# Decoder middle by token half, later helical end and second experts' opening in another order: one core of Trainium2

## The reference, cut to what matters

```python
x = x + cross_attention(layernorm(x), ctx)               # 257 keys per sequence, gelu instead of softmax
x = x + rwkv(layernorm(x))
x = x + experts0(layernorm(x))                           # 1 shared and 7 routed, two chosen
x = x + decoder(layernorm(x), ctx)                       # below
x = x + helical_attention(layernorm(x))                  # 16 heads
x = x + experts1(layernorm(x))                           # 16 experts, three chosen

def decoder(y, Z):
    y = layernorm(y + attention(y, y, y, causal=True), g1, beta1)
    y = layernorm(y + attention(y, Z, Z), g2, beta2)
    return layernorm(y + relu(y @ w1 + b1) @ w2 + b2, g3, beta3)
```

## Time and profile before

| what | us |
|---|---|
| median of three runs | 596.7 |
| the profiled execution, its own time | 599.34 |
| its span | 597.5 |
| first experts end, decoder begins | 243 |
| helical units begin | 330 |
| second norm half of the second experts turned | 468.6 |
| first `down` of the second experts | 496.7 |
| the steps' last product, then the end | 591.8, 597.5 |
| PE / DVE / ACT / POOL busy | 458 / 424 / 299 / 103 |

### The profile page before, as it was taken

The page is one execution under the profiler, slowest core; times in us unless marked ns, Lnnn a source line. Parts: engine busy times, 40 slices in busy tenths (PEclk is TensorE's granted clock), DMA queues, the critical chain, the costliest instruction groups (busy, mean ns, idle before and its releaser), DMA issues.

```text
span 597.5 us, 8935 instructions
## 1 busy us (share of the span) xinstructions
PE 458.3 (77%) x2922; PEld 346.8 (58%) x2939; DVE 423.7 (71%) x1013; ACT 299.4 (50%) x555; POOL 103.4 (17%) x104
## 2 busy tenths in 40 slices
PE   5754233999999999454667789999864349999996
PEld 2331232777787777342434678888763327777774
DVE  3369856777777776546879797878765457888885
ACT  4135031777666665232222566765632107777774
POOL 1000012222111220000044211222100320332220
PEclk9867555999999999755877989999985559999999
DMA  8930001110111100000000000000001000111101
GB/s 318 420 148 0 0 1 53 54 43 11 53 53 53 53 15 2 0 0 1 2 0 2 2 1 2 2 2 1 2 1 35 21 20 31 37 39 66 35 0 36
DMA packets 7422, 24.08 MB, mean 40 GB/s; under 512 B 774, under 2 KB 2998, under 8 KB 7260
## 3 DMA queue, kind: packets, MB, share of 16 engines
q1 hardware_dynamic: 7388, 23.63, 10.8%
HBM read 23.11 MB, written 0.52 MB: 40 GB/s over the span
## 4 chain that ended last, share of the span: by engine, by line
PE 58%; DVE 19%; issue 8%; ACT 7%; DMA 3%; SPq 2%; POOL 1%; DVEq 0%; POOLq 0%; ACTq 0%
PE pair L321 13%; PE pair L323 13%; PE pair L322 13%; DMA mb<-in_mb 3%; PE turn L315 2%; PE pair L640 2%; PE turn L321 1%; DVE st L1129 1%; PE pair L372 1%; DVE work L1313 1%; PE turn L322 1%; DVE arena L1480 1%; PE turn L323 1%; SPq L280 1%; ACT YT L762 1%
## 5 line engine op out<-in xcount | busy, mean ns | idle before, releaser
L994 ACT ACTIVATE work<-pair,vec 128x512 f32<-128x512 f32 x64 | 44.0, 688 | 39.1 <-PE pair L323 33.2
L321 PE MATMUL pair<-yTh,wh 128*128 128x512 f32 x128 | 61.4, 480 | 0.0
L1581 DVE TENSOR_TENSOR pair<-work,turn 128x512 f32<-128x512 f32 x64 | 44.5, 696 | 20.2 <-ACT work L994 18.9
L322 PE MATMUL pair<-yTl,wh 128*128 128x512 f32 x128 | 51.4, 401 | 0.0
L323 PE MATMUL pair<-yTh,wl 128*128 128x512 f32 x128 | 51.3, 401 | 0.0
L1351 DVE TENSOR_TENSOR pair<-work,pair 128x512 f32<-128x512 f32 x48 | 33.4, 696 | 24.1 <-PE pair L323 23.4
L1042 POOL TENSOR_TENSOR wl<-wraw,wh 128x512 fp32r<-128x512 f32 x24 | 30.9, 1291 | 99.3 <-ACT wh L831 99.3
L852 ACT ACTIVATE ph<-pair 128x512 fp32r<-128x512 f32 x48 | 28.7, 599 | 27.4 <-DVE pair L1351 27.4
L839 ACT ACTIVATE work<-pair 128x512 f32<-128x512 f32 x64 | 38.2, 598 | 4.8 <-PE pair L323 3.6
L321 PE MATMUL pair<-ph,wh 128*128 128x512 f32 x96 | 38.2, 398 | 1.1 <-DVE pl L1369 0.8
L640 PE MATMUL pair<-arena 64*128 64x128 f32 x512 | 34.8, 289 | 4.7 <-ACT work L918 4.5
(11 more groups left out here) (276 smaller groups left out, 1239.2 us busy)
## 6 DMA issues: line engine op xcount, KB each, us to landing
wraw<-in_w SPq DMA_DIRECT2D x8, 768.0 KB, 4.2
arena<-in_zT SPq DMA_DIRECT2D x8, 514.0 KB, 10.3
arena<-in_z SPq DMA_DIRECT2D x8, 512.0 KB, 11.1
wraw<-in_w SPq DMA_DIRECT2D x8, 512.0 KB, 3.2
mat<-in_mat SPq DMA_DIRECT2D x1, 2571.5 KB, 18.8
row<-in_row SPq DMA_DIRECT2D x1, 576.0 KB, 18.6
X<-in_x SPq DMA_DIRECT2D x1, 512.0 KB, 4.1
out_x<-X SPq DMA_DIRECT2D x2, 256.0 KB, 2.5
```

The costliest lines, as they stand in the source:

```text
L321: pe.matmul(out, ah, bh, start=start, stop=False)
L322: pe.matmul(out, ah, bl, start=False, stop=False)
L994: act.activation(act_out[q % 2], UP1[q % 4], ACT.Relu, bias=vec[:, bass.ds(at, 1)])\
L1581: dve.tensor_tensor(UP1[q % 4], act_out[q % 2], bank[h], ALU.mult).then_inc(m["mul"], 1)
```

## The change

In the decoder, norms 1 and 2 are made for each half by itself. Half 0 starts cross-attention while half 1 is normalised between tiles 0 and 2; half 1 is turned at tile 2; half 0 is normalised and turned again behind tiles 6 and 7. POOL's helical preparation starts as soon as the decoder's opening norm is done. At the helical end unit 7's two score passes come ahead of unit 6's softmax sum and weighing, and the first half's last norm is split into statistics and a later rest. In the second experts the logits are made by half into another bank, the first three `up` come before the gates, the bias product comes behind the gates' transposes, and ACT makes the gates' float copy. `route` (L370) is cut into `logits` and `turn_gates`; `cross` calls the function it is given behind `turn_probs(t)` on PE, and between `result(t - 2)` and `top(t + 2)` on DVE. The diff, cut to its core:

```diff
@@ PE
             def moe1():
-                pe.wait_ge(m_g3, 4)
-                pe.wait_ge(y_lo, 6)
-                for h in range(2):
-                    pe.matmul(acc[h], mb2[:, :], g3f[:, h * HN:(h + 1) * HN], start=True, stop=False)
                 pe.sem_inc(m["down"], FREE1["down"])
...
+                pe.wait_ge(y_lo, 6)
                 for q in range(3):
                     up(0, q)
+                pe.wait_ge(m_shift, 2)
+                for h in range(2):
+                    pe.matmul(acc[h], zerob[:, :], g3b[:, h * HN:(h + 1) * HN], start=True, stop=False)
+                turn_gates(3 * NE1, 1)
+                for h in range(2):
+                    pe.wait_ge(m_g3, 3 + h)
+                    spread(0, 2 * h)
+                for h in range(2):
+                    pe.wait_ge(m_gf, h + 1)
+                    pe.matmul(acc[h], mb2[:, :], g3f[:, h * HN:(h + 1) * HN], start=False, stop=False)
...
-            pe.wait_ge(feat_ready, n)
-            pe.wait_ge(a_y2, 2)
-            cross(1)
+            def other_turns(t):
+                if t == 2:
+                    pe.wait_ge(feat_ready, turn_half(1))
+                if t == NT:
+                    turn_half(0)
+            pe.wait_ge(feat_ready, turn_half(0))
+            cross(1, other_turns)
...
-                if u >= 2:
+                if u >= 2 and u != 8:
                     turn_weights(u - 2)
                 if 1 <= u <= len(HEL):
                     score(u - 1, 0)
+                if u == 8:
+                    turn_weights(6)
+                    score(7, 1)
...
-                if u == 9:
-                    pe.wait_ge(h_o, 7)
-                    turn4(lambda i: Y[:, i, :])
-                    pe.wait_ge(feat_ready, 18)
                 if u >= 2:
                     weigh_values(u - 2)
-                if 1 <= u <= len(HEL):
+                if 1 <= u < len(HEL):
                     score(u - 1, 1)
...
-            pe.wait_ge(h_x, 2)
-            n = turn4(lambda i: Y[:, HT + i, :])
-            pe.wait_ge(feat_ready, n)
-            route("gate", NE1, 3 * NE1, 1)
+            for h in range(2):
+                if h == 1:
+                    pe.wait_ge(h_x, 2)
+                n = turn4(lambda i: Y[:, h * HT + i, :])
+                pe.wait_ge(feat_ready, n)
+                logits("gate", NE1, 1, range(h * HT, (h + 1) * HT))
             moe1()
@@ ACT
                                accum_out=ssum[:, t:t + 1]).then_inc(c_probs, 1)
-            inverse_std(0, 1)
+                if t == 2:
+                    copy_turned(yt(1))
+            inverse_std(0)
...
-                    if h == 1 and f == 0:
-                        inverse_std(0)
+                    if f == 0:
+                        inverse_std(1 - h)
...
+                if u == 8:
+                    extract(7, 0)
...
+            for h in range(2):
+                act.wait_ge(m_g3, 3 + h)
+                c = slice(h * HN, (h + 1) * HN)
+                act.activation(g3f[:, c], g3b[0:3 * NE1, c], ACT.Copy).then_inc(m_gf, 1)
@@ POOL
-            pool.wait_ge(f_h, 1)
+            pool.wait_ge(tok_ready, 8)
@@ DVE
-                    if call == 1:
-                        dve.tensor_copy(g3f[:, c], src)
...
-            layernorm((0, 1), Y2, Y2, lambda h: affine(h, Y2, "g1", "be1").then_inc(tok_ready, 1))
-            dve.wait_ge(tok_ready, 12)
-            cross(1)
-            layernorm((0, 1), Y2, Y2, lambda h: affine(h, Y2, "g2", "be2").then_inc(tok_ready, 1))
+            norm1(0, attended(0))
+            var[1] = attended(1)
+            def other_norms(t):
+                if t == 0:
+                    norm1(1, var[1])
+                if t == 6:
+                    dve.wait_ge(c_x, NT + HT)
+                    norm2(0, statistics((0,), Y2))
+            cross(1, other_norms)
+            norm2(1, statistics((1,), Y2))
...
+                if u == 8:
+                    extract(7, 0)
                 if u >= 2:
                     softmax_sum(u - 2)
+                if u == 9:
+                    var[0] = statistics((0,), X)
...
+                if u == 8:
+                    extract(7, 1)
+                    softmax_shift(7)
                 if u >= 2:
                     result(u - 2)
...
-                if u == 8:
-                    layernorm((0,), X, Y)
+            normal((0,), X, Y, var[0])
             add_out(1)
```

More of the change, by code:

```diff
@@ L323, in mm3, with cross @@
                 return pe.matmul(out, al, bh, start=False, stop=stop)
-            def cross(call):
+            def cross(call, between=None):
                 def scores(t):
@@ L364, in cross @@
                         turn_probs(t)
+                    if between is not None:
+                        between(t)
                     if t + 2 < NT:
@@ L368, in cross, with logits, turn_gates @@
                         weigh(t - 1)
-            def route(name, ne, rows, call):
-                for t in range(NT):
-                    last = pe.matmul(bank[2][:, t * NE1:t * NE1 + ne], blk(YT, t), mcol(name), start=True, stop=True)
+            def logits(name, ne, call, tiles):
+                for t in tiles:
+                    last = pe.matmul(LOGITS[call][:, t * NE1:t * NE1 + ne], blk(YT, t), mcol(name), start=True, stop=True)
                 last.then_inc(m_logits, 1)
+            def turn_gates(rows, call):
+                pe.wait_ge(m_parts, call + 1)
                 for h in range(2):
-                    pe.wait_ge(m_parts, call + 1)
                     for i in range(HT):
-                        last = pe.transpose(blk(bank[3 + h].bitcast(BF16), i)[0:rows, :],
+                        last = pe.transpose(blk(GATES_T[call][h].bitcast(BF16), i)[0:rows, :],
                                             parts_of(rows // 3)[:, h * HT + i, :], identb[:, :])
@@ L492, in body @@
                         if not last or q + 3 < len(STEPS1):
+                            if (q + 3) % NF1 == 0:
+                                spread(i, q + 3)
                             up(i, q + 3)
@@ L534, in _ @@
             pe.wait_ge(feat_ready, n)
-            route("router", NE0 - 1, 3 * NE0, 0)
+            logits("router", NE0 - 1, 0, range(NT))
+            turn_gates(3 * NE0, 0)
             moe0()
@@ L875, in _ @@
                                           scale=scale, accum_out=ssum[:, t:t + 1])
[L876 to L881, removed]
+                last.then_inc(tok_ready, 1)
+                if h == 0:
+                    copy_turned(spT(0))
+            copy_turned(spT(1))
+            inverse_std(0)
+            copy_turned(yt(0))
+            inverse_std(1)
             for t in range(NT):
@@ L1250, in routing_parts, with add_experts @@
                     dve.wait_ge(m_gT, 2 * call + h + 1)
-                    src = bank[3 + h].bitcast(BF16)[0:3 * w, 0:HN]
+                    src = GATES_T[call][h].bitcast(BF16)[0:3 * w, 0:HN]
                     c = slice(h * HN, (h + 1) * HN)
-                    if call == 1:
-                        dve.tensor_copy(g3f[:, c], src)
                     dve.tensor_copy(g3b[0:3 * w, c], src).then_inc(m_g3, 1)
-            def moe_end(m):
-                for h in range(2):
-                    dve.wait_ge(m["back"], h + 1)
-                    dve.tensor_tensor(half(X, h), bank[2 + h], half(X, h), ALU.add).then_inc(m["x"], 1)
+            def add_experts(m, h):
+                dve.wait_ge(m["back"], h + 1)
+                dve.tensor_tensor(half(X, h), bank[2 + h], half(X, h), ALU.add).then_inc(m["x"], 1)
             dve.wait_ge(x_loaded, 16)
@@ L1376, in _ @@
             bodies(dve, NE0 // 2, body0)
-            moe_end(m)
-            dve.wait_ge(m["x"], 2)
-            layernorm((0, 1), X, Y)
+            var = [0, 0]
+            for h in range(2):
+                add_experts(m, h)
+                dve.wait_ge(m["x"], h + 1)
+                var[h] = statistics((h,), X)
+            for h in range(2):
+                normal((h,), X, Y, var[h])
             for h in range(2):
@@ L1390, in _, with attended @@
                 hs = slice(h * HT, (h + 1) * HT)
-                dve.wait_ge(a_prob, h + 1)
-                dve.sem_inc(tok_ready, 1)
+                dve.wait_ge(tok_ready, 9 + h)
                 step(dve.reciprocal(ssum[:, hs], ssum[:, hs]))
-            for h in range(2):
+            def attended(h):
                 dve.wait_ge(a_out, h + 1)
```

115 lines of the change are left out of this document (63 added, 52 removed).

## The result

| | before | after |
|---|---|---|
| median of the runs, us | 596.7 | **575.47** (four runs, 574.63 to 576.51) |
| the profiled execution, its own time | 599.34 | 576.51 |
| its span, mean granted clock | 597.5, 0.849 | 574.7, 0.863 |

The ratio to before is 0.964, 95% interval 0.9618 to 0.9662: 21.2 us faster by the medians, where 18.6 were forecast.

The account below looks back on a forecast made before the run. Expert stages and helical units were taken as bound by TensorE, handoffs by one engine working while the rest wait. Decoder -8.2, helical end -8.4 and opening -2.0 sum to -18.6: from 596.7 to 578.1 us, range 569.5 to 585.

Parts of the forecast that it names:

- Rival (a): Whole change: the port costs nothing and the clock rises as today; at most -30.1 us, middle about 569.7; chance 0.15.
- Rival (b): Inserted norms only move DVE's work; decoder -3.7, opening +0.4, helical -8.4, so 585 us; chance 0.17.
- Rival (c): Slower: smaller TensorE bursts between waits keep it at half clock; 22 us of such work give 600; chance 0.03.
- Rival (d): Decoder halves bring nothing, only POOL's earlier start gains; -14.6, so 582 us; chance 0.1 of the forecast's.
- the mixed sums: Two of decoder -13.5, helical -9.5, opening -7.1 with the forecast of the third: -25.0 to -29.0 us.
- L1429: Second half's small tensor_scalar in the decoder's opening norm: taken as blocked by POOL until about 261.1, 2.7 us late.
- Cross-attention: Decoder: starts at 271.0 instead of 278.04 and lasts 29.3 us, between 26.3 and 29.3, against 17.6 today.
- I take half clock for four more tiles: In cross-attention, TensorE idling during the inserted norm delays the clock's rise: 4 x (2.51 - 1.76) = 3.0 us.
- the hidden 0.7: In cross-attention, 0.7 us of the half-clock addition of 3.0 that the inserted norm hides.
- Feed-forward: Decoder: POOL's blocking goes, L1426 starts at 311.2, 6.9 us earlier; helical turn at 321.4, today 329.55.
- Helical end: Unit 7's weighing starts 9.4 us earlier; the last turn comes 8.4 earlier; ends -6.5 and -9.5.
- Opening: Second experts: logits -1.8, gate chain +4.1, gates to first `down` -4.3; together -2.0 us, ends -7.1 and +0.4.

Follow-up runs that it names:

- POOL late: The changed kernel with one wait put back, so POOL starts its helical preparation at the first feed-forward product again: 581.53 us, ratio 0.9752.
- the helical end and the opening alone: Two kernels, each the kernel before with one part: the helical end's new order, 590.06 us; the second experts' opening, 595.42 us.
- the second execution of the change: A second profiled execution of the changed kernel, nothing altered, from its repeat as yardstick: median 576.12 us, ratio 0.9644.
- the helical fill: The changed kernel plus 19 unused zero products on TensorE, 7 ahead of the helical turn and 12 behind the projections: 573.73 us, ratio 0.9599.
- the split held: The changed kernel with POOL's second weight split held until the gates' transposes, here with 18 zero products ahead of them: 569.96 us, ratio 0.9542.
- the kernel with all three edits: The changed kernel with POOL's second split held and zero products both ahead of the gates' transposes and around the helical turn: 567.94 us, ratio 0.9507.

## Why the prediction was right, and where it was not

- **Sign, size, mechanism.** 578.1 was forecast and 575.47 measured, inside the range; of the named cases the forecast itself came in. Rival (a), -30.1, and (b), -11.7, stay out on both sides. Rival (b) gave the decoder -3.7, and the helical turn came 13.0 earlier, with L593 8.6 earlier than before (forecast 3.9). Rival (c) falls with the sign, though the clock did take something, below. Rival (d), that the halves bring nothing, falls with POOL late: some 15 of the 21 us remain, where the helical end and the opening alone give 9.2.
- **How much of it is luck.** The traces have -10.0, -7.9 and -2.0 where the forecast had -8.2, -8.4 and -2.0. The decoder's number is near because two misses partly cancel: cross-attention was priced 3.6 too high, and the clock behind the helical turn, 2.7 in this execution, was not priced at all. The opening's is exact by two misses of about 0.8 that cancel. (In rival (a) the lowest of the mixed sums is -24.8, not -25.0; no case changes by it.)
- **L1429.** The second half's was taken as 2.7 late and lost 1.60; the first half's, not in the forecast, lost 0.55. The mechanism is the forecast one, since both end with a POOL instruction. The size was too large because POOL's casts and splits were shorter here than beside the feed-forward: the wide split ended 8.8 us after POOL's start (247.90 to 256.73) and not 10.3. L1439 came at 261.7 comparable, forecast 263.0, and cross-attention at 269.8, forecast 271.0.
- **Cross-attention: the term that was mis-sized.** It was given 29.3 us, and took 25.7 (292.62 - 266.90); in all ten profiled executions with this order and no fill here it took 25.7 to 26.9. The two rates were right: ACT's exponentials are 2.50 apart at half clock (277.87 to 280.37) and 1.81 at full (280.37 to 282.18), 2.51 and 1.76 in the forecast. What failed is the step "I take half clock for four more tiles". The clock was up for the rest of the tiles only 13.6 us after the start (280.5), where before it was 8.9, but by then most tiles were through: before, the step from the fourth tile's exponential to the fifth's was the last at half clock, after it was the next one. So in this execution one more tile was paid at half clock, 0.75 us, and not four. Without the addition for the clock the sum was 27.0, less the hidden 0.7 it was 26.3. Why the clock rose in between and fell back, no run here settles.
- **Feed-forward.** L1482 comes 10.3 behind L593 (forecast 10.9), its casts 0.42 (0.5), so the whole of the 4.7 by which L593 beat its forecast (1.2 of it from the earlier start, 3.6 from cross-attention) arrived: L1482 at 305.9 comparable, forecast 311.2, and the helical turn 13.0 earlier, forecast 8.2.
- **A term that was missing.** Of these 13.0, 3.0 were given back by the first unit's values, 2.7 of them by the first bias product: TensorE, idle for long stretches around the turn, ran the projections and the first dots at half clock. In the second execution of the change the turn came only 10.9 earlier and 1.3 were given back. The forecast had put no price on the clock there; the helical fill measures it (2.4).
- **Helical end.** L694 for unit 7 and the last turn came 8.4 and 7.9 earlier, forecast 8.5 and 8.4. The 0.7 for POOL's rest on the small steps is L1186 at 0.78 instead of 0.16.
- **Opening.** The gate chain grew by 3.3 (14.3 against 11.0), forecast 4.1: four splits and their casts lengthened five of DVE's steps (to 0.96, 1.17, 0.59, 1.23 and 0.91; before, the first was 0.47, the second, a copy, 0.23 and the others 0.29). The logits gave 1.7 (1.8), and from the gates' transposes to the first `down` 4.4 were won (11.72 before, 7.32 after). Of these 0.8 went back at once, since the second `down` follows at 2.52 and not 1.74: 3.6 in all, forecast 4.3. Net -2.0 in the trace, as forecast; alone, 1.2 with an interval that touches zero.

## What to carry to other kernels

When DVE and GpSimd get in each other's way and one has free work to place, look for the place where the other runs its smallest instructions: in this kernel the same splits cost 2.2 us beside two small steps, some 4 more beside a norm, and 6 more beside a norm's products and the bias tiles. And where a handover leaves TensorE idle, the products behind it may be paid at half clock, as at the helical turn and behind the gates, so that the gain of a shorter handover and the clock behind it are two separate terms; where nothing useful can be put into the gap, unused products can be worth their place (8.2 us here, with one split held back), as long as they end before the real work is due.

## What was not expected of the hardware

- Products of zeros keep the granted clock up. 24 of them brought the bias products from 3.78 to 1.98 us. One of 512 columns takes 0.24 us (5.82 / 24).
- A fill can be too long. With the split held, 18 products took 4.69 from 461.40, the chain was over at 465.23, and the gates' transposes began at 466.02: 0.8 us lost. In the kernel with all three edits the same 18 took 4.05 and nothing was lost, the transposes coming 14.39 behind the logits.
- TensorE busy for 8.99 of 9.20 us can still be at half clock (the last row of the table after), while the clock rose for a part of a stretch in which it was 7.02 of 9.60 us busy (the first row, 0.65). The busy share of a stretch doesn't tell its clock.
- The beginning of the decoder, 240 us into the kernel, lies anywhere from 238.6 to 243.2 over fourteen executions with the same code ahead of it. A trace's differences are to be taken between marks inside it, not from its start.
